# Moving a filter network's first layer into a counting stage, and its buffers with it

## The reference

```
# layer 0: how many edges lead from s to d: the aggregation is then a matrix product with the counts
agg = segment_sum(xn[src], dst); mean = agg / max(deg, 1)
h = mean @ W_l + b + xn @ W_r; h = h * sigmoid(h)
# layer 1: a filter for each edge from its 20 radial features f_ij
h   = softplus(f_ij @ W1 + b1) - log(2)          # 32 hidden units
Wij = (h @ W2 + b2) * rcut_ij[:, None]           # 128 of the 192 columns are needed
```

## Time and profile before

| | |
|---|---|
| median of 3 runs | 2703.25 us (2703.01 to 2705.48) |
| profiled execution, its own time | 2706.97 us |
| its span, first to last instruction | 2705.2 us |
| busy: PE, DVE, ACT, POOL | 93%, 67%, 34%, 63% of the span |
| chain that ended last, by engine | PE 80%, DVE 7%, issue 5%, DMA 4%, POOL 3%, ACT 1% |
| DMA `filters<-filt` on that chain | 2% |
| POOL `AT` (L648) on that chain | 1% |
| mean granted TensorE clock | 0.937 |

### The profile page before, as it was taken

How to read it: one execution, slowest core, us unless ns; L and a number is a source line. 1 busy time by engine, 2 the same in 40 slices (tenths; PEclk the granted TensorE clock), 3 DMA queues, 4 the chain that set the end, 5 groups by cost and what they waited for, 6 DMA issues and landing times.

```text
span 2705.2 us, 35016 instructions
## 1 busy us (share of the span) xinstructions
PE 2510.5 (93%) x11808; PEld 2104.0 (78%) x11808; DVE 1803.3 (67%) x2638; ACT 917.4 (34%) x1111; POOL 1691.4 (63%) x755
## 2 busy tenths in 40 slices
PE   6877997898879976999999999999999999999998
PEld 6866887777769975777777777777777777777776
DVE  8754332464668956777777777777777777777774
ACT  1254112452238953222222222232222222223221
POOL 1342402223888854777777777777777777777773
PEclk9977977798779987999999999999999999999999
DMA  2013102002132221122122122212212212221211
GB/s 67 2 62 148 47 0 78 0 1 67 41 109 81 86 66 36 63 93 93 62 93 93 70 85 93 85 70 93 93 62 93 93 69 86 93 85 70 93 62 35
DMA packets 48881, 190.90 MB, mean 71 GB/s; under 512 B 12292, under 2 KB 16903, under 8 KB 32436
## 3 DMA queue, kind: packets, MB, share of 16 engines
q1 hardware_dynamic: 34720, 177.90, 18.0%
q0 software_dynamic: 13200, 10.75, 1.7%
q10 hardware_dynamic: 900, 1.44, 0.2%
HBM read 177.54 MB, written 12.35 MB: 70 GB/s over the span
## 4 chain that ended last, share of the span: by engine, by line
PE 80%; DVE 7%; issue 5%; DMA 4%; POOL 3%; ACT 1%; SPq 0%; DVEq 0%; POOLq 0%; ACTq 0%
PE PS L1656 24%; PE PS L1658 24%; PE PS L1657 24%; PE PS L1923 3%; PE PS L1924 2%; DMA filters<-filt 2%; POOL AT L648 1%; POOL gatW L704 1%; POOL XN L704 1%; DVE negmax L1337 1%; DMA X<-in_x 0%; DVE PTl L1354 0%; DVE XN L1057 0%; PE PS L1881 0%; DVE XTl L1066 0%
## 5 line engine op out<-in xcount | busy, mean ns | idle before, releaser
L1605 DVE SCALAR_TENSOR_TENSOR XN<-PS,attn,XN 125x512 f32<-125x512 f32 x1083 | 805.7, 749 | 441.1 <-PE PS L1658 432.4
L742 POOL TENSOR_TENSOR OPl<-TS,OPh 128x1024 fp32r<-128x1024 f32 x256 | 677.1, 2645 | 117.1 <-ACT OPh L1003 117.1
L742 POOL TENSOR_TENSOR OPl<-RAW,OPh 128x1024 fp32r<-128x1024 f32 x192 | 555.2, 2892 | 274.8 <-ACT OPh L1003 274.7
L1656 PE MATMUL PS<-OPh,XTh 128*125 128x512 f32 x1280 | 507.5, 396 | 2.0 <-DVE attn L1559 2.0
L1658 PE MATMUL PS<-OPh,XTl 128*125 128x512 f32 x1280 | 506.1, 395 | 0.0
L1657 PE MATMUL PS<-OPl,XTh 128*125 128x512 f32 x1280 | 503.6, 393 | 0.0
L1003 ACT ACTIVATE OPh<-TS 128x1024 fp32r<-128x1024 f32 x256 | 271.8, 1062 | 529.3 <-PE PS L1658 519.4
L1656 PE MATMUL PS<-OPh,Sh 128*125 128x512 f32 x1024 | 404.9, 395 | 3.4 <-DVE XN L1602 3.4
L1658 PE MATMUL PS<-OPh,Sl 128*125 128x512 f32 x1024 | 404.1, 395 | 0.0
L1657 PE MATMUL PS<-OPl,Sh 128*125 128x512 f32 x1024 | 402.7, 393 | 0.0
L1003 ACT ACTIVATE OPh<-RAW 128x1024 fp32r<-128x1024 f32 x192 | 203.9, 1062 | 581.1 <-PE PS L1658 581.1
(11 more groups left out here) (358 smaller groups left out, 3746.5 us busy)
## 6 DMA issues: line engine op xcount, KB each, us to landing
RAW<-in_values SPq DMA_DIRECT2D x64, 2048.0 KB, 7.5
filters<-filt SPq DMA_DIRECT2D x14, 750.0 KB
fil<-filters SPq DMA_DIRECT2D x11, 937.5 KB
Wraw<-in_ffn SPq DMA_DIRECT2D x4, 1024.0 KB, 5.3
Wraw<-in_L_q SPq DMA_DIRECT2D x2, 1024.0 KB, 9.5
Wraw<-in_L_k SPq DMA_DIRECT2D x2, 1024.0 KB, 7.8
Wraw<-in_L_v SPq DMA_DIRECT2D x2, 1024.0 KB, 8.8
gatW<-nodes,dstI POOLq DMA_INDIRECT x90
```

Of the source, the lines that this page charges most:

```text
L742: g.tensor_tensor(OPl[:, j], operand_source(j, parity), OPh[:, j].bitcast(F32), ALU.subtract).then_inc(op_lower, 1)
L1605: v.scalar_tensor_tensor(out=XN[:, t], in0=PS[0:P, bank, :], scalar=w, in1=XN[:, t], op0=ALU.mult, op1=ALU.add).then_inc(v_added, 1)
L1656: mm(dst, lh, rh, start=start, stop=False, skip_group_check=resumed)
```

## The change

- The count's chunks 1 to 7 now each carry one pair of the filter network: TensorE runs its first layer behind the chunk, ScalarE its softplus (the ReLU too, now on ScalarE), and GpSimd the sum. All 14 steps' hidden units stay in a new buffer `hidden_h` (28 KB a partition).
- Behind the count remain, for each of 14 steps, the rounding, the remainder, the second layer, the scaling and the store, written out without a loop.
- GpSimd's split of weight 0 stands behind the seventh pair's sum, ahead of the last two windows. ScalarE's split of `AT` comes after step 3 (`SPLIT_AFTER`), VectorE's scaling of `AT` ahead of the first filter tile.
- `ATh` and `ATl` now lie over the one-hot buffers, and `iotaI` shares its place with `fields`; `relu_h` is gone. The buffers behind them keep their places.

```diff
-F_START = NCH - 3
+F_FIRST = 1
+SPLIT_AFTER = FPAIRS // 2
...
-            ATh = sb("ATh", [P, T, NT], F32R, area)
-            ATl = sb("ATl", [P, T, NT], F32R, area)
             with ExitStack() as s:
                 hotS = sb("hotS", [P, 2, CH, N + 1], BF16, s)
...
+                hidden_h = sb("hidden_h", [GROUPS * F, FSTEPS, FT * P], F32, s)
+            ATh = sb("ATh", [P, T, NT], F32R, area)
+            ATl = sb("ATl", [P, T, NT], F32R, area)
...
+        def pair_behind(c):
+            return c - F_FIRST if 0 <= c - F_FIRST < FPAIRS else None
...
@@ GpSimd
+            for c in range(NCH):
+                m = c // COUNT_CHUNKS
+                if c == count_end(m):
...
+                j = pair_behind(c)
+                if j is not None:
+                    for i in range(2):
+                        n = 2 * j + i
+                        pool.wait_ge(f_ln, n + 1)
+                        g.tensor_tensor(hidden_h[:, n], hidden_h[:, n], soft[:, i], ALU.add).then_inc(f_hidden, 1)
+                if j == FPAIRS - 1:
+                    split_weight(0)
             pool.wait_ge(f_padded, 1)
+            for n in range(FSTEPS):
+                pool.wait_ge(f_upper, n + 1)
+                if n >= 2:
+                    pool.wait_ge(f_second, 2 * n - 2)
+                g.tensor_tensor(hTl[0:GROUPS * F, n % 2], hidden_h[:, n], hTh[0:GROUPS * F, n % 2].bitcast(F32), ALU.subtract).then_inc(f_lower, 1)
@@ ScalarE
-            def logarithms(j):
+            def softplus(j):
...
-                    if not before(j, 1):
+                    if j > 0:
                         act.wait_ge(f_hidden, n - 1)
-                    a.activation(soft[:, i], PS[0:GROUPS * F, 6 + i, 0:FT * P], ACT.Abs, bias=b1c[:, 0:1]).then_inc(f_abs, 1)
+                    z = PS[0:GROUPS * F, 6 + i, 0:FT * P]
+                    a.activation(soft[:, i], z, ACT.Abs, bias=b1c[:, 0:1]).then_inc(f_abs, 1)
+                    a.activation(hidden_h[:, n], z, ACT.Relu, bias=b1c[:, 0:1]).then_inc(f_relu, 1)
...
+            for c in range(NCH):
...
+                if pair_behind(c) is not None:
+                    softplus(pair_behind(c))
             act.wait_ge(f_padded, 1)
+            for n in range(FSTEPS):
+                act.wait_ge(f_hidden, n + 1)
...
+                a.activation(hTh[0:GROUPS * F, n % 2], hidden_h[:, n], ACT.Copy).then_inc(f_upper, 1)
+                if n == SPLIT_AFTER:
+                    act.wait_ge(at_final, 1)
+                    a.activation(ATh[:, :, 0:2 * HALF], AT[:].rearrange("p t h n -> p t (h n)"), ACT.Copy).then_inc(at_upper, 1)
@@ VectorE
-                if c == F_START + 1:
-                    dve.wait_ge(f_consts, F_CONSTS)
-                    relu_step(0, 0)
-                    relu_step(0, 1)
-                    hidden_pair(0)
...
+            for n in range(FSTEPS):
+                i = n % 2
+                if n >= 2:
+                    dve.wait_ge(f_stored[i], 16 * (n // 2))
+                for h in range(2):
+                    dve.wait_ge(f_second, 2 * n + h + 1)
...
@@ TensorE
-                if c == F_START:
+                if c == F_FIRST:
                     pe.wait_ge(f_consts, F_CONSTS)
-                    first_layer(0)
+                if pair_behind(c) is not None:
+                    first_layer(pair_behind(c))
...
+            for n in range(FSTEPS):
+                pe.wait_ge(f_lower, n + 1)
+                for h in range(2):
+                    if n:
+                        pe.wait_ge(f_scaled, 2 * n + h - 1)
```

More of the change, by code:

```diff
@@ L531, in _ @@
                 radial_load(sp, i, i)
[L533 to L538, removed]
+            for n in range(FSTEPS):
+                i, g = n % 2, GROUPS * FT
+                sp.wait_ge(f_scaled, 2 * n + 2)
+                sp.dma_start(filters[:, n * g:(n + 1) * g, :], filt[:, i].rearrange("p s (g f) -> p (s g) f", f=128)).then_inc(f_stored[i], 16)
             load_weight(1)
@@ L637, in _ @@
             g.tensor_tensor(W2l[:], W2d[:], W2h[:].bitcast(F32), ALU.subtract).then_inc(f_inputs, 1)
[L639 to L648, removed]
@@ L651, in _ @@
[L651 to L661 removed]
+            for c in range(NCH):
+                m = c // COUNT_CHUNKS
+                if c == count_end(m):
+                    for s in range(T):
+                        n = T * m + s
+                        pool.wait_ge(unpacked, n + 1)
+                        f = fields[:, n % 2]
+                        if m == 0:
+                            g.tensor_copy(AT[:, s], f).then_inc(added, 1)
+                        else:
+                            pool.wait_ge(added, n - 4)
+                            g.tensor_tensor(AT[:, s], AT[:, s], f, ALU.add).then_inc(added, 1)
+                j = pair_behind(c)
[6 more added lines that the diff above has]
+                    split_weight(0)
@@ L798, in logarithms @@
                     act.wait_ge(f_exp, 2 * j + i + 1)
+                    act.wait_ge(f_relu, 2 * j + i + 1)
                     a.activation(soft[:, i], soft[:, i], ACT.Ln, scale=0.5, bias=halfc[0:GROUPS * F, 0:1]).then_inc(f_ln, 1)
[L801 to L813, removed]
@@ L814, in _ @@
-            act.wait_ge(f_padded, 1)
[L816 to L825, removed]
@@ L1103, in _ @@
             transposed_rest("xt0")
[L1106 to L1120, removed]
             for c in range(NCH):
@@ L1147, in _ @@
             v.memset(hTl[GROUPS * F:GROUPS * F + 1].bitcast(F32), 0.0).then_inc(f_padded, 1)
[L1148 to L1156, removed]
-                        r = factor[:, bass.ds(n * 2 * GROUPS, 2 * GROUPS), :].rearrange("p (s g) k -> p s (g k)", s=2)
-                        v.tensor_tensor(filt[:, i, 2 * h:2 * h + 2].rearrange("p s (m f) -> p s m f", f=F),
-                                        PS[0:P, 2 * h:2 * h + 2, 0:GROUPS * 128].rearrange("p s (m f) -> p s m f", f=F),
-                                        r.unsqueeze(3).to_broadcast([P, 2, 4 * GROUPS, F]), ALU.mult).then_inc(f_scaled, 1)
-                    if i == 0 and not (isinstance(j, int) and j == FPAIRS - 1):
-                        relu_step(j + 1, 0)
-                        relu_step(j + 1, 1)
-                if not (isinstance(j, int) and j == FPAIRS - 1):
-                    hidden_pair(j + 1)
-            for_pairs(dve, filter_pair)
             dve.wait_ge(added, T * COUNTS)
@@ L1713, in first_layer @@
                     pe.wait_ge(radial_loaded[i], 16 * (j + 1))
-                    if not before(j, 1):
+                    if j > 0:
+                        pe.wait_ge(f_abs, n - 1)
                         pe.wait_ge(f_relu, n - 1)
@@ L1735, in _ @@
             pe.wait_ge(f_padded, 1)
-            def filter_pair(j):
-                if not (isinstance(j, int) and j == FPAIRS - 1):
-                    first_layer(j + 1)
-                for i in range(2):
-                    pe.wait_ge(f_lower, 2 * j + i + 1)
-                    for h in range(2):
-                        n = 2 * (2 * j + i) + h
-                        if not (before(j, 1) and i == 0):
-                            pe.wait_ge(f_scaled, n - 1)
-                        for b in (2 * h, 2 * h + 1):
-                            c = tile_columns(b)
-                            ins = product(PS[0:P, b, 0:GROUPS * 128], (hTh[:, i, c], hTl[:, i, c]), (W2h[:], W2l[:]), True, True)
-                        ins.then_inc(f_second, 1)
-            for_pairs(pe, filter_pair)
+            for n in range(FSTEPS):
+                pe.wait_ge(f_lower, n + 1)
+                for h in range(2):
+                    if n:
+                        pe.wait_ge(f_scaled, 2 * n + h - 1)
+                    for b in (2 * h, 2 * h + 1):
+                        c = tile_columns(b)
+                        ins = product(PS[0:P, b, 0:GROUPS * 128], (hTh[:, n % 2, c], hTl[:, n % 2, c]), (W2h[:], W2l[:]), True, True)
+                    ins.then_inc(f_second, 1)
             pe.wait_ge(f_scaled, 2 * FSTEPS)
```

36 lines of the change are left out of this document (23 added, 13 removed).

## The result

The changed kernel takes **2719.41 us** (median of 4 runs, 2716.36 to 2723.43), the kernel before, run beside it, 2704.36 us. The ratio is 1.0057, with a 95% interval of 1.0039 to 1.0074: slower by 15.1 us, where 8.9 were forecast, and above the top of the range (2718). Timed again, the same kernel gave 1.0046 (1.0031 to 1.0062): 12.5 us by this ratio, 14.1 between the two medians.

What follows compares the result with a forecast made beforehand. VectorE was taken to bound the count and the stores the filter stage. Terms 10.8 + 8.2 - 1.6 - 4.9 - 3.6 = +8.9 us on 2703.25 gave 2712.2 us, range 2700 to 2718.

Steps and rivals of the forecast that it cites:

- Hidden additions in the count: Count windows: GpSimd's two additions a pair hold VectorE's one-hots, 1.8 us a pair, +10.8 us for six pairs.
- Split and seventh pair: Count, chunk 9: weight 0's split with the seventh pair's additions holds VectorE as one piece, +8.2 us.
- ReLU pair out of the count: Count's last windows: ReLU pair and its additions no longer stand between two unpackings, -1.6 us.
- TensorE covered: Count windows: two first layers make 26.3 us of TensorE against 25 + 3.6, so VectorE covers them.
- rival A: Count: GpSimd's additions don't hold VectorE, so the kernel gets faster, 2693 to 2699 us; chance 0.12.
- ScalarE covered: Count: softplus and two ReLUs, 7.8 us in a chunk of 14, cost zero, but tight.
- Gap: Between count and first store: the first lower half no longer waits for weight 0's split, -4.9 us.
- Stage: Filter stage: feature loads leave; twelve stores take 71.4 us plus 1.5 to get going, instead of 76.6, -3.6 us.
- behind 252.8 all is as before, only later: After the last scaled filter tile (252.8 us): nothing changes except that it comes later.
- B: Count: 1.0 us lost a pair, 6.5 for the split; no measurable difference, +2.4, 2705.7 us; chance 0.18.
- C: Count: full durations of GpSimd's instructions, or delayed ScalarE rounding, +12.5 to +15, 2716 to 2718 us; chance 0.13.
- late rounding: Count: softplus ends about when VectorE wants the first rounded tile; bound 1 us in each of three windows.

Runs made afterwards that it cites:

- a_short_adds: Changed kernel with GpSimd adding one column of each step's logarithms instead of all 500: 2710.98 us, ratio 1.0010 to the kernel before.
- a_split_stage: Changed kernel with only the split of weight 0 moved out of the count, behind the sixth lower half: 2713.13 us, ratio 1.0022 to the kernel before.
- a_late_adds: Changed kernel with 14 logarithm buffers, additions behind the count and the weight 0 split in the stage: 2700.53 us, ratio 0.9972 to the kernel before.
- a_loads: Changed kernel with the twelve radial loads issued again in the filter stage, unread: 2726.02 us (1 run).
- a_again: Changed kernel, no edit, timed again: 2720.91 us, ratio 1.0046 to the kernel before.
- b_split_stage: Kernel before with only the split of weight 0 moved behind the first pair's lower halves: 2706.69 us, ratio 0.9991.
- late_wide: Changed kernel with additions behind the count, weight 0 split in the stage, each store cut into 120 and 5 rows: 2669.93 us, ratio 0.9869 to the kernel before.

## Why the prediction was right in sign and too small

By its own steps, from the profiled pair:

1. *Hidden additions in the count*, forecast +10.8 for six pairs: measured 3.94, 3.86 and 3.88 in three windows, **+11.7**. One addition takes 1.22 us (a pair 2.44), not 1.15, and VectorE lost 1.94 us a pair, not 1.8. a_short_adds shows the cause. The Trainium skill ("SBUF — State Buffer", section "Who interferes with whom") has the lock held for the whole instruction. The trace agrees in kind: one-hots end with the GpSimd instruction beside them. In size it shows 1.94 of 2.44 us and 8.1 of 9.0, the rest being the held one-hots' own work.
2. *Split and seventh pair*, forecast +8.2: the fourth window grew by 8.1 (33.2 against 25.1). a_split_stage gives 6.4 for the split alone.
3. *ReLU pair out of the count*, forecast -1.6. The last stretch of the count took 8.4 us instead of 9.4, so **-1.0**.
4. *TensorE covered*: right, and with less room than was thought. Two chunks and two first layers make 24.5 us, not 26.3, and the windows without a hold take 24.5 to 25.1. The price that was set for the case without cover (up to 1.5 us a window, up to 6 in rival A) was too high; a_late_adds has no hold, and only its first window is longer than before, by 0.45 us.
5. *ScalarE covered*: right. Windows with its full 19.9 us are 24.5 to 25.1 long in a_late_adds.
6. *Gap*, forecast -4.9: **-4.6**.
7. *Stage*, forecast -3.6: **-4.9**. a_loads gives 3.2 to the loads. The loop's 1.6 us between landings and stores stood in no term. The twelfth landing came 71.7 us behind the first store, so the 1.5 us that the sum had for getting going, on top of 71.4 for the stores, weren't there. The statement behind it, that the rest is hidden by stores on 5 engines, is shown by the kernels with cut stores.

Forecast and measured sum differ by little in the three parts: +18.8 - 4.6 - 4.9 = +9.3 against +8.9. Some of this is luck: the count was forecast 1.4 us too low and the gap's gain 0.3 too high, and the stage's gain was 1.3 too low. The step that failed is the frame of the sum: "behind 252.8 all is as before, only later", and nothing ahead of the first window's end. Both were put at zero without a reason, and the measured time lies 15.1 us up, or 12.5 to 14.1 in the second timing, where the parts hold 9.3. In the profiled pair 1.3 us lie ahead (the first window ended at 53.0 instead of 51.7) and 0.9 behind the last filter tile; with the 9.3 these are the 11.5 of the pair.

The rest isn't in the pair, and it is not this kernel's alone. The five timings of kernels with whole stores and the layers moved lie above their dates each time:

| | by the three parts | by the medians | excess |
|---|---|---|---|
| after | +9.3 | +15.1 | 5.8 |
| a_again | +9.1 | +14.1 | 4.9 |
| a_split_stage | +2.8 | +6.3 | 3.5 |
| a_short_adds | -3.0 | +4.1 | 7.1 |
| a_late_adds | -9.8 | -6.3 | 3.5 |
| b_split_stage | -3.7 | -1.6 | 2.2 |

Each difference of medians is uncertain by 2 to 4 us, and four of these rows share their runs of the kernel before; still, five excesses of one sign speak for a cost outside the three parts. The row of b_split_stage, with nothing moved but the split, is above its dates too, and the three kernels with cut stores and the moved layers don't show it (-3 to +2 us, with the earlier `XWh` counted). What it is stays open. The first window's end varies from 51.1 to 54.7 us over the twelve profiles, in kernels with and without the change. One hint: the three profiles without the moved layers have 2 long gather issues each, the nine with them have 2 to 6, on average 3.3; three profiles are too few to call that shown. The range had been made from the terms' bounds alone, with nothing for the spread of the medians or for the untouched stages; that was too narrow at the top.

Rival A (VectorE not held) is refuted by the one-hots of 1.31 and 4.31 us, B (partial holds) too: of a pair 1.94 us were lost, not 1.0, and 8.1 in the window with the split, not 6.5. C's whole durations give 12.4, which is close to the second timing's ratio by luck: the additions and the split cost 19.8 us and not 22.5, and its late rounding didn't occur.

## What to carry to other kernels

Work that is moved onto an idle engine is free only if that engine doesn't hold up the one that sets the pace: look for the instruction of the pacing engine that is three times as long as its neighbours. Here the work was free where VectorE's instructions read PSUM, as long as the stores set the pace; with cut stores GpSimd's own 6.4 us stood on the chain. Before taking work out of a stage, see what the stage waits for: here the stores hid all of it but the loads and the loop's steps, and cutting 125 rows into 120 and 5 was worth more than anything the change gained (12 us in the kernel before, 28 with the late additions, by the ratios). And where single runs of an untouched stage differ by 13 us, compare the dates of the touched parts.

## What was not expected of the hardware

Stores of 125 rows and 750 KB kept a DMA share of 0.32, about 5 engines; cut into 120 and 5 rows the share was 0.58 to 0.75 over the stage, and a store's piece on the chain took 4.5 us where that of the earlier trace rows, which starts behind another store, took 9.76. While such a piece runs, the share is higher (late_wide):

```profile
207.20:211.70 4.50, 3.56 (x19) 2.95 (x18) 1.82 (x2) 0.62 (x1) 3.77 (x4) 1.00 0.84 227
```

These shares (5 of 16 engines are 0.31, 15 of 16 are 0.94) agree with the Trainium skill ("DMA: Bandwidth & Descriptors", section "Why a DMA increments its semaphore by 16 and not by 1"), by which 125 rows use 5 engines and 120 rows spread over 15.

Gather issues on GpSimd took now 1.5 us and now 4.6, the latter 2 to 6 times among the 165 of an execution; profiles with 4 or 6 long ones took 3 us or a little more for each beyond two in the message stage, those with 3 took 0 to 4 us more.
